# Attention in 64-token chunks with two carried states per tile, and a new order of the work around them

## The chip, the core and the metric

One core of a Trainium2 chip runs the whole program. The metric is the device time of one execution in microseconds (us), lower is better; the median of three runs is given. TensorE does the matrix products, VectorE and ScalarE read their results from the accumulation memory (PSUM, eight banks of 512 fp32 values per partition), GpSimd scatters rows with indirect DMAs, SyncE issues plain DMAs. Every engine runs its own list of instructions in order, and waits on semaphores that the others count up. In the profile TensorE is PE, VectorE DVE, ScalarE ACT, GpSimd POOL.

## The reference

Two residual blocks on X of shape (2, 2048, 256). The first is linear attention with 16 heads of width 16; the second routes each token to 4 of 32 experts, beside a shared expert. The change is in the first block alone:

```python
K = X.reshape(B, L, H, d)          # X here is the layer-normed input, B=2, L=2048, H=16, d=16
Q = rms_norm_multihead((X @ Wq.T).reshape(B, L, H, d), q_norm_w)
V = rms_norm_multihead((X @ Wv.T).reshape(B, L, H, d), v_norm_w)
W = jnp.cumsum(jnp.einsum('blhd,blhe->blhde', K, V), axis=1)    # a running 16x16 state per head
out = jnp.einsum('blhd,blhde->blhe', Q, W).reshape(B, L, D)
x = x + out
```

## The kernel before, in words

The 4096 tokens are 32 tiles of 128. Each engine runs a function `step` once per round; in round i the block `tile_of(k)` works on tile i-k, so a round does one stage of several tiles. The order of the blocks in `step` is the order on that engine, written by hand; nothing reorders it. Channels come in two groups (g) of 128, each of four blocks (j) of 32 channels, which is two heads (r).

For a tile t the stages are, with their lines on TensorE:

- `xn`, the normed tile (ScalarE L517), is transposed (L785), and copied to `xnT` (ScalarE L533). The QV product makes Q and V before their norm, 512 columns in bank `pQV` (L828, two products).
- The norm of Q and V: squares on ScalarE (`sq`, L571), sums per head on VectorE (L1152), logarithm and exponential on ScalarE (L594, L602: a first guess of the root), then three small VectorE operations (L1191, L1202, L1216) give the factors `rr`. VectorE scales Q to `qn` (L1234) and V to `vp` (L1240).
- `qn` is transposed (L817), ScalarE makes from it `qm` (Q masked to one head of each pair, L556) and `qT` (L562).
- The scores, key by query within the tile, are products of 32 rows by 128 columns (L795) into the four banks `pS0` to `pS3`. A causal mask `tri` is applied in three banks by VectorE (L1089), in the fourth by a ScalarE copy (L527) and a GpSimd operation (L482).
- The output of the tile is the product of `qT` with the state carried so far, `w_bd` (L869), plus the masked scores times V (L888), both in bank `pO`. The state sum is added to in bank `pT1` (L877), and VectorE masks it into `w_bd` (L1180) for the next tile.
- ScalarE scales the output to `oT` (L614), TensorE transposes it (L803), VectorE adds it to x (L1113). After that come the second norm and the router of the experts (L774, L838, L846, L858 and many small VectorE operations), and GpSimd scatters each tile's rows four times (L467).

On TensorE the order in a round is: L774, L785, L795 (tile i-2), L803 (tile i-3), L817 (tile i-1), L828 (tile i), router, L869, L877, L888 (tile i-2). On ScalarE `oT` of tile i-3 is the last thing in a round, behind the logarithm and the guess of tile i-1.

Then come the shared expert and 144 blocks of the routed experts, and the sums of their outputs, which the change leaves as they are.

## Time and profile before

| | |
|---|---|
| median of 3 runs | 559.55 us (555.07 to 562.66) |
| the profiled execution: its own time | 559.33 us |
| its span, first to last instruction | 557.4 us |
| PE busy | 527.4 us (95%) |
| DVE / ACT / POOL busy | 382.2 / 376.5 / 331.8 us |
| attention stage | about 10 to 215 us of the span |

The profile is one execution. Times are microseconds from the span's start, unless marked ns. A matrix product of fp32 operands shows as two instructions (x16 for eight products), a transpose as one. "128*32" beside a matrix product is the shape of the part of the array it uses, rows by columns; several such parts can hold products at the same time. Durations of neighbours on an engine may overlap, so what an instruction takes of its engine's time is better read from one start to the next.

### The profile page before, as it was taken

The page shows a single profiled execution, that of the slowest core. Times are in us where ns is not written, and L with a number is a line of the kernel's source. Part 1 is how long each engine was busy: PE and PEld are TensorE (multiplying, and loading weights), DVE is VectorE, ACT ScalarE, POOL GpSimd, SP SyncE. Part 2 cuts the span into 40 slices and gives each one's busy share as a digit, 9 for nine tenths or more (in the row PEclk, how much of TensorE's full clock was granted, in tenths as well). Part 3 has the DMA queues.
Part 4 walks back from the last instruction along what each step waited for, and adds up shares of the span by engine and source line. Part 5 has one row for each costly group of instructions (what it writes and reads, how often), then busy time and mean ns, then how long its engine had stood idle before and what let it go on. Part 6 is the DMA issues. An engine that isn't in the chain of part 4 may idle for free.

```text
span 557.4 us, 18176 instructions
## 1 busy us (share of the span) xinstructions
PE 527.4 (95%) x5177; PEld 383.1 (69%) x5177; DVE 382.2 (69%) x1354; ACT 376.5 (68%) x1258; POOL 331.8 (60%) x367
## 2 busy tenths in 40 slices
PE   6798999999999999699999999999999999997996
PEld 2355666666666665357998988999999995544554
DVE  7698999999999996664444444444444446744786
ACT  2687899988989985402766766777677776653452
POOL 6010377776777777771665555666666564446992
PEclk8999999999999999899999999999999999998999
DMA  8998355556456554954676776766666554428999
GB/s 259 316 292 264 125 217 211 187 215 227 186 198 246 188 192 152 366 194 127 195 219 201 221 225 199 214 193 194 194 193 198 180 187 145 143 79 342 408 409 347
DMA packets 65088, 123.29 MB, mean 221 GB/s; under 512 B 9824, under 2 KB 44000, under 8 KB 64992
## 3 DMA queue, kind: packets, MB, share of 16 engines
q1 hardware_dynamic: 47824, 78.07, 44.1%
q0 software_dynamic: 13056, 39.86, 19.2%
q10 hardware_dynamic: 4112, 4.19, 2.3%
q8 instruction: 45, 0.74, 0.6%
q14 instruction: 51, 0.42, 0.3%
HBM read 58.49 MB, written 63.60 MB: 219 GB/s over the span
## 4 chain that ended last, share of the span: by engine, by line
PE 79%; DMA 5%; DVE 4%; issue 4%; ACT 3%; POOL 2%; SPq 1%; ACTq 1%; DVEq 0%; POOLq 0%
PE pS L967 18%; PE pQV L828 10%; PE pS L985 9%; PE pS L741 8%; PE pS L795 5%; PE pO L888 5%; DMA xg<-xs 3%; PE pO L869 3%; PE pT L946 3%; PE pQV L946 2%; PE pQV L757 2%; PE pO L757 2%; PE pT L774 2%; PE pO L803 2%; PE pT L817 1%
## 5 line engine op out<-in xcount | busy, mean ns | idle before, releaser
L495 POOL DMA_INDIRECT ys<-gsh,dst x144 | 138.1, 959 | 108.3 <-ACT gsh L663 86.6
L467 POOL DMA_INDIRECT xs<-xg,posi x128 | 123.8, 967 | 52.1 <-issue 31.4
L967 PE MATMUL pS<-after_a,x2T_all 128*128 128x128 f32 x1024 | 135.5, 276 | 0.0
L967 PEld LDWEIGHTS pS<-after_a,x2T_all 128*128 128x128 f32 x1024 | 124.5, 192 | 0.0
L1375 DVE TENSOR_TENSOR after_a<-after_a,pS 128x128 f32<-128x128 f32 x144 | 41.5, 288 | 79.9 <-ACT after_a L651 76.1
L1346 DVE COPY x2T_all<-w 128x512 f32 x144 | 63.9, 444 | 32.9 <-issue 32.5
L985 PE MATMUL pS<-w,after_a 128*128 x256 | 76.7, 381 | 0.0
L1089 DVE TENSOR_TENSOR w<-pS,tri 128x512 f32<-128x512 f32 x96 | 65.1, 679 | 1.0 <-PE pS L795 1.0
L828 PE MATMUL pQV<-w 128*128 128x512 f32 x128 | 63.7, 621 | 0.5 <-ACT w L533 0.5
L663 ACT ACTIVATE gsh<-pS,xg 128x256 f32<-128x256 f32 x128 | 60.6, 474 | 0.4 <-issue 0.4
L662 ACT CAST dst<-xg 128x1 int32 x128 | 24.5, 191 | 45.3 <-PE pS L985 43.3
L741 PE MATMUL pS<-x2T_all,ws 128*128 128x512 f32 x104 | 50.6, 636 | 1.3 <-ACT sg L624 0.7
L651 ACT ACTIVATE after_a<-pS 128x128 f32<-128x128 f32 x144 | 40.1, 279 | 16.5 <-PE pS L967 10.7
L482 POOL TENSOR_SCALAR_AFFINE_SELECT w<-w 128x512 f32<-128x512 f32 x32 | 20.6, 643 | 43.3 <-ACT w L527 43.0
L500 POOL TENSOR_TENSOR w<-w 128x512 f32<-128x512 f32 x32 | 40.7, 1272 | 7.7 <-DMA w<-ys 7.4
L985 PEld LDWEIGHTS pS<-w,after_a 128*128 128x128 f32 x256 | 38.9, 192 | 0.4 <-issue 0.4
L556 ACT ACTIVATE w<-pT,mwq 128x128 f32<-128x128 f32 x128 | 36.8, 379 | 1.9 <-PE pT L817 1.7
L741 PEld LDWEIGHTS pS<-x2T_all,ws 128*128 128x128 f32 x104 | 20.9, 207 | 24.6 <-issue 24.3
L795 PE MATMUL pS<-w 32*128 32x256 f32 x512 | 36.7, 401 | 0.0
L828 PEld LDWEIGHTS pQV<-w 128*128 128x128 f32 x128 | 22.2, 194 | 20.2 <-issue 18.2
L888 PE MATMUL pO<-w 128*32 128x128 f32 x1024 | 34.6, 274 | 1.3 <-POOL w L482 0.6
L647 ACT COPY after_a<-pT 128x256 f32<-128x256 f32 x72 | 26.1, 363 | 11.4 <-PE pT L946 11.3
(221 smaller groups left out, 1019.8 us busy)
## 6 DMA issues: line engine op xcount, KB each, us to landing
xg<-xs SPq DMA_DIRECT2D x128, 160.0 KB, 2.8
ys<-gsh SPq DMA_DIRECT2D x32, 512.0 KB
w<-ys SPq DMA_DIRECT2D x32, 512.0 KB, 15.3
w<-in_L_ffn_W ACTq DMA_DIRECT2D x1, 4096.0 KB, 18.6
out<-xall SPq DMA_DIRECT2D x14, 256.0 KB, 7.2
xs<-padrow SPq DMA_DIRECT2D x32, 80.0 KB
xg<-xs SPq DMA_DIRECT2D x32, 80.0 KB, 2.2
ys<-gsh,dst POOLq DMA_INDIRECT x144
```

The source lines that it names most:

```text
L467: pool.indirect_dma_start(out=xs, out_offset=bass.IndirectOffsetOnAxis(ap=posi[:, a.r8, k:k + 1], axis=0), in_=xr[:, a.r8, :], in_offset=N ...
L495: pool.indirect_dma_start(out=ys, out_offset=bass.IndirectOffsetOnAxis(ap=dst[:, j % 8:j % 8 + 1], axis=0), in_=y[:, j % 8, :], in_offset= ...
L663: act.activation(y[:, a.r8, :], pS[2 + a.b][:, 0:D], ACT.Copy, scale=xg[:, a.r8, bass.ds(e[0] + D, 1)]).then_inc(S["y_done"], 1)
L741: last = pe.matmul(h_bank(g, m, n)[:], ws13[:, k, n, m * P:(m + 1) * P], x2T_all[:, k, g * TG:(g + 1) * TG], start=(k == 0), stop=(k == KC ...
L795: last = pe.matmul(pS[j][:, g * 256:(g + 1) * 256], xnT[32 * j:32 * j + 32, a.r3, g, :], qm[32 * j:32 * j + 32, :, g, :], start=(g == 0), ...
L828: last = pe.matmul(pQV[:], xnT[:, a.r3, k, :], wqv[:, k, :], start=(k == 0), stop=(k == KC - 1))
L888: last = pe.matmul(pO[32 * j:32 * j + 32, g * P:(g + 1) * P], vp[:, a.b, 4 * g + j, r:r + 2, :], s_sb[:, j, g, r, :], start=False, stop=(r ...
L967: last = pe.matmul(pS[a.b][:, n * P:(n + 1) * P], w13_staged(a.t)[:, (2 * k + n) * F:(2 * k + n + 1) * F], xgT[:, a.b, k, :], start=(k == ...
L985: last = pe.matmul(pS[2 + a.b][:, 0:D], geT[:, a.b, :], w2_of(e), start=True, stop=True)
L1089: dve.tensor_tensor(s_sb[:, j].rearrange("p g r l -> p (g r) l"), pS[j][:].rearrange("p (n l) -> p n l", l=P), tri[:].unsqueeze(1).to_broa ...
L1346: dve.tensor_copy(w13_staged(j), w13[:, bass.ds(staged_of(j), 1), :, :, :].rearrange("p a k n f -> p (a k n f)")).then_inc(S["w13_staged"], 1)
L1375: dve.tensor_tensor((ge if mixed(a.t) else geT)[:, a.b, :], sge[:, a.b, :], pS[a.b][:, F:2 * F], ALU.mult).then_inc(S["ge_done"], 1)
```

## The change

Each tile of 128 tokens is treated as two chunks (c) of CH = 64 tokens. Scores are made within a chunk only, so they are half as many: products of 32 rows by 64 columns with 128 streamed columns (L805 of the changed kernel), into the first 256 columns of the four banks, now one tensor `pS_all`. The mask is two VectorE operations of two banks each (L1100); the ScalarE copy and the GpSimd mask are gone. The state is carried twice per tile: `carry(b, 0)` for the first chunk and `carry(b, 1)` for the second, each 128 columns (VectorE, L1114), and `add_to_state` adds one chunk (64 rows) to the sum in `pT1`. The product with the carried states and the product of scores and V are of 64 rows by 32 columns with 64 streamed columns (L880, L890). The output goes to the second halves of banks 2 and 3, the transposed `qn` to that of bank 1 (`pQT`), the transposed output to that of bank 0 (`pOT`); the QV product alternates between the banks `pQV` and `pO`, and is issued in two halves with the transposes of `qn` between them. `xn` has four buffers instead of three. On ScalarE `normalise` and `xr` (L552) move forward, and `oT` moves ahead of the logarithm and the guess. On VectorE `v_done` (scaling V) moves from the end of a round into the next.

TensorE, one round before (in it a tile's router columns, L846 to L858):

```order
L774 MATMUL pT<-ident,xg 128x128 x2
L785 MATMUL pT<-ident,w 128x128 x2
L795 MATMUL pS<-w 128x256 x8
L803 MATMUL pO<-ident,w 128x128 x2
L817 MATMUL pT<-ident,w 128x128 x2
L828 MATMUL pQV<-w 128x512 x2
L846 MATMUL pT<-mask,tri 128x64
L847 MATMUL pT<-mcum,ones 128x64
L858 MATMUL pT<-x2T_all,wg 32x128 x4
L869 MATMUL pO<-w,w_bd 32x128 x8
L877 MATMUL pT<-w 32x32 x8
L888 MATMUL pO<-w 32x128 x16
```

and the same round of the changed kernel, which starts behind the state sum of the first chunk (L763, the row that ends it here):

```order
L781 MATMUL pT<-ident,xg 128x128 x2
L793 MATMUL pT<-ident,w 128x128 x2
L805 MATMUL pS<-w 64x128 x16
L814 MATMUL pQV<-w 128x512
L821 MATMUL pS<-ident,w 128x128 x2
L828 MATMUL pQV<-w 128x512
L834 MATMUL pS<-ident,w 128x128 x2
L854 MATMUL pT<-mask,tri 128x64
L855 MATMUL pT<-mcum,ones 128x64
L865 MATMUL pT<-x2T_all,wg 32x128 x4
L763 MATMUL pT<-w 32x32 x8
L880 MATMUL pS<-w,w_bd 32x64 x16
L890 MATMUL pS<-w 32x64 x32
L763 MATMUL pT<-w 32x32 x8
```

The transposes of the output (L834) have moved behind the QV product, the QV product is split, and the state sum of the second chunk stands ahead of the product with the carried states (L880), that of the next tile's first chunk behind the last product (L890).

ScalarE, the part of a round from the squares on, before:

```order
L571 ACTIVATE w<-pQV 128x512
L576 COPY rk<-pT 128x64
L585 COPY after_a<-pT 128x128
L517 ACTIVATE w<-xall,nb,rr 128x256
L594 ACTIVATE lnm<-ss,eps_col 128x34
L602 ACTIVATE guess<-lnm 128x34
L614 ACTIVATE w<-pO,wvc 128x128 x2
L533 COPY w<-pT 128x256
```

and in the changed kernel:

```order
L569 ACTIVATE w<-pQV 128x512
L574 COPY rk<-pT 128x64
L583 COPY after_a<-pT 128x128
L590 ACTIVATE w<-pS,wvc 128x128 x2
L599 ACTIVATE lnm<-ss,eps_col 128x34
L607 ACTIVATE guess<-lnm 128x34
L531 COPY w<-pT 128x256
```

The two operations that make `oT` (L614, now L590) have moved from behind the guess to ahead of the logarithm (L594, now L599).

The core of the diff:

```diff
-        pS = [pb(f"pS{j}") for j in range(4)]
+        pS_all = ctx.enter_context(nc.psum_tensor("pS", [P, 4, 512], F32))
+        pS = [pS_all[:, j, :] for j in range(4)]
+        pQT, pOT = pS_all[:, 1, 256:512], pS_all[:, 0, 256:512]
+        pO_chunks = pS_all[:, 2:4, 256:256 + KC * CH].rearrange("p c (g l) -> p c g l", g=KC)
...
+        def carry(b, c):
+            return w_bd[:, b, c * P:(c + 1) * P].rearrange("p (g j e) -> p g j e", g=KC, j=2)
...
-                if (a := tile_of(2)) is not None:
-                    pool_wait(S["s_copied"], banks_copied(a.t) + 1)
-                    v = s_sb[:, 1].rearrange("p g r l -> p (g r) l")
-                    pool.affine_select(out=v, in_=v, compare_op=ALU.is_ge, fill=0.0, base=0,
-                                       pattern=[[0, 4], [1, P]], channel_multiplier=-1).then_inc(S["masked_pool"], 1)
...
-                if (a := tile_of(3)) is not None:
-                    copy_scores(a, 1)
+                if (a := tile_of(0)) is not None and a.t > 1:
+                    normalise(a.t)
...
+                if (a := tile_of(3)) is not None:
+                    wait(act, S["o_ps"], a.t + 1)
+                    wait(act, S["ot_ps"], a.t)
+                    if a.t == 0:
+                        act.wait_ge(S["wc_in"], 64)
+                    for g in range(KC):
+                        last = act.activation(oT[:, g, :].rearrange("p (c l) -> p c l", c=2), pO_chunks[:, :, g, :], ACT.Copy,
+                                              scale=wvc[:, g:g + 1])
+                    last.then_inc(S["oT_done"], 1)
                 if (a := tile_of(1, LAG)) is not None:
...
+            def add_to_state(a, c):
+                wait(pe, S["v_done"], a.t + 1)
+                wait(pe, S["carried"], states_summed(a.t, c))
+                for g in range(KC):
+                    for j in range(4):
+                        last = pe.matmul(pT1[32 * j:32 * j + 32, g * 2 * d:(g + 1) * 2 * d],
+                                         xn[c * CH:(c + 1) * CH, a.r4, g * P + 32 * j:g * P + 32 * j + 32],
+                                         vp[c * CH:(c + 1) * CH, a.b, 4 * g + j, 0:3:2, :],
+                                         start=(a.t % NTB == 0 and c == 0 and g == 0), stop=True, skip_group_check=True)
+                last.then_inc(S["state_ps"], 1)
...
                     wait(pe, S["qm_done"], a.t + 1)
-                    wait(pe, S["masked"], banks_masked(a.t))
-                    wait(pe, S["s_copied"], banks_copied(a.t))
+                    wait(pe, S["qT_done"], a.t + 1)
+                    wait(pe, S["oT_done"], a.t)
+                    wait(pe, S["x2_done"], a.t - 1)
                     for g in range(KC):
+                        for c in range(2):
+                            for j in range(4):
+                                last = pe.matmul(pS[j][c * CH:(c + 1) * CH, g * P:(g + 1) * P],
+                                                 xnT[32 * j:32 * j + 32, a.r3, g, c * CH:(c + 1) * CH],
+                                                 qm[32 * j:32 * j + 32, :, g, c * CH:(c + 1) * CH],
+                                                 start=(g == 0), stop=True, skip_group_check=True)
+                    last.then_inc(S["scores_ps"], 1)
...
+                if (a := tile_of(0)) is not None:
+                    wait(pe, S["xnT_done"], a.t + 1)
+                    wait(pe, S["qn_done"], a.t - 1)
+                    wait(pe, S["v_done"], a.t - 1)
+                    pe.matmul((pQV, pO)[a.b][:], xnT[:, a.r3, 0, :], wqv[:, 0, :], start=True, stop=False)
...
                         keep_busy(2, 512)
                     wait(pe, S["qn_done"], a.t + 1)
-                    wait(pe, S["x2T_done"], a.t - 3)
-                    wait(pe, S["xnT_done"], a.t + 2, NT)
+                    wait(pe, S["masked"], scores_masked(a.t - 1) + 1)
                     for g in range(KC):
-                        last = pe.transpose(pT0[:, g * P:(g + 1) * P], qn[:, a.b, g * P:(g + 1) * P], ident[:])
+                        last = pe.transpose(pQT[:, g * P:(g + 1) * P], qn[:, a.b, g * P:(g + 1) * P], ident[:])
                     last.then_inc(S["qT_ps"], 1)
...
+                    pe.matmul((pQV, pO)[a.b][:], xnT[:, a.r3, 1, :], wqv[:, 1, :], start=False, stop=True).then_inc(S["qv_ps"], 1)
+                if (a := tile_of(3)) is not None:
+                    wait(pe, S["oT_done"], a.t + 1)
+                    wait(pe, S["masked"], scores_masked(a.t + 1) + 1, scores_masked(NT))
+                    wait(pe, S["x2_done"], a.t)
+                    for g in range(KC):
+                        last = pe.transpose(pOT[:, g * P:(g + 1) * P], oT[:, g, :], ident[:])
...
+                if (a := tile_of(2)) is not None and a.t < NT - 1:
+                    add_to_state(a, 1)
                 if (a := tile_of(2)) is not None:
                     wait(pe, S["qT_done"], a.t + 1)
-                    wait(pe, S["state_done"], a.t)
-                    wait(pe, S["x2_done"], a.t)
+                    wait(pe, S["carried"], states_summed(a.t, 1))
+                    wait(pe, S["masked"], scores_masked(a.t + 1))
                     for g in range(KC):
+                        for turn in range(2):
+                            for j in range(4):
+                                i = j // 2
+                                c = (i + turn) % 2
+                                last = pe.matmul(pO_chunks[32 * j:32 * j + 32, c, g, :], carry(a.b, c)[i * CH:(i + 1) * CH, g, j % 2, :],
+                                                 qT[i * CH:(i + 1) * CH, a.b, g, c * CH:(c + 1) * CH],
+                                                 start=(g == 0), stop=False, skip_group_check=True)
                     last.then_inc(S["o1_ps"], 1)
                 if (a := tile_of(2)) is not None:
-                    wait(pe, S["v_done"], a.t + 1)
-                    wait(pe, S["masked"], banks_masked(a.t + 1))
-                    wait(pe, S["masked_pool"], banks_copied(a.t + 1))
+                    pe.wait_ge(S["o1_ps"], a.t + 1)
                     for g in range(KC):
                         for r in range(2):
+                            for c in range(2):
+                                for j in range(4):
+                                    last = pe.matmul(pO_chunks[32 * j:32 * j + 32, c, g, :],
+                                                     vp[c * CH:(c + 1) * CH, a.b, 4 * g + j, r:r + 2, :],
+                                                     s_sb[c * CH:(c + 1) * CH, j, g, r, :],
+                                                     start=False, stop=(r == 1), skip_group_check=True)
                     last.then_inc(S["o_ps"], 1)
+                if (a := tile_of(1)) is not None:
+                    add_to_state(a, 0)
+                if (a := tile_of(2)) is not None and a.t == NT - 1:
+                    pe.wait_ge(S["carried"], states_summed(NT - 1, 1))
+                    shared_half(1, 1, 0)
...
-            def mask_scores(a, j):
-                wait(dve, S["scores_ps"], 4 * a.t + j + 1)
+            def mask_scores(a, half):
+                banks = slice(2 * half, 2 * half + 2)
+                wait(dve, S["scores_ps"], a.t + 1)
                 wait(dve, S["o_ps"], a.t)
+                dve.tensor_tensor(s_sb[:, banks].rearrange("p j g r l -> p j (g r) l"),
+                                  pS_all[:, banks, 0:4 * CH].rearrange("p j (n l) -> p j n l", l=CH),
+                                  tri[:, 0:CH].unsqueeze(1).unsqueeze(1).to_broadcast([P, 2, 4, CH]), ALU.mult).then_inc(S["masked"], 1)
+
+            def carry_state(t, c):
+                if c == 0:
+                    wait(dve, S["state_ps"], states_summed(t))
+                    wait(dve, S["o1_ps"], t - 1)
+                else:
+                    wait(dve, S["state_ps"], states_summed(t, 1))
+                    wait(dve, S["o1_ps"], t - 1)
+                if c == 0 and t % NTB == 0:
+                    dve.memset(carry(t % 2, 0), 0.0).then_inc(S["carried"], 1)
+                else:
+                    dve.tensor_tensor(carry(t % 2, c),
+                                      pT1[:, 0:KC * 2 * d].rearrange("p (g e) -> p g e", g=KC).unsqueeze(2).to_broadcast([P, KC, 2, 2 * d]),
+                                      head_mask[:, :, 0:CH].rearrange("p g (j e) -> p g j e", j=2), ALU.mult).then_inc(S["carried"], 1)
 
             def step(tile_of):
                 if (a := closing(tile_of(9))) is not None:
...
+                if (a := tile_of(2)) is not None:
+                    wait(dve, S["rms_done"], a.t + 1)
+                    wait(dve, S["o_ps"], a.t - 1)
+                    wait(dve, S["state_ps"], states_summed(a.t - 1))
+                    dve.tensor_tensor(vp[:, a.b, :, 0:3:2, :], (pQV, pO)[a.b][:, D:2 * D].rearrange("p (n r e) -> p n r e", r=2, e=d),
+                                      rr[:, a.b, H:2 * H].rearrange("p (n r) -> p n r", r=2).unsqueeze(3).to_broadcast([P, NP_, 2, d]),
+                                      ALU.mult).then_inc(S["v_done"], 1)
+                if (a := tile_of(3)) is not None:
+                    carry_state(a.t, 1)
+                if (a := tile_of(3)) is not None:
+                    mask_scores(a, 1)
...
+                if (a := tile_of(3)) is not None and a.t < NT - 1:
+                    carry_state(a.t + 1, 0)
```

## Rows read from the trace of the kernel before

**Rows 1.** Windows: length, busy us of PE, PEld, DVE, ACT, POOL, clock, DMA, GB/s

```profile
100.00:120.00 20.00, 19.98 (x326) 13.20 (x314) 19.54 (x91) 18.02 (x63) 14.48 (x16) 1.00 0.55 202
...
220.00:240.00 20.00, 14.76 (x48) 7.02 (x45) 13.76 (x75) 8.44 (x27) 14.95 (x16) 0.83 0.94 334
```

**Rows 2.** Chain of waits, 82.3 to 198.4 us, by line

```profile
by line: PE pQV L828 30.4%; PE pS L795 17.6%; PE pO L888 15.8%; PE pO L869 8.2%; PE pT L774 6.4%; PE pO L803 6.0%; PE pT L817 3.7%; PE pT L785 3.6%; PE pT L858 3.1%; PE pT L877 2.0%; PE pT L846 1.6%; PE pT L838 1.5%; PE pT L847 0.2%; issue 
```

**Rows 3.** Line L785, 80 to 200 us: durations, first and last start

```profile
L785 PE MATMUL pT<-ident,w x40: 272/273/273, 82.3 to 198.4; 128*128 128x128 f32 x40
```

**Rows 4.** Timeline of PE, 133 to 141.4 us: start, us, instruction

```profile
133.05 1.96 PE L828 MATMUL pQV<-w 128*128 128x512 f32 x4
135.01 0.19 PE L846 MATMUL pT<-mask,tri 128*128 128x64 f16 x1
...
135.40 0.62 PE L869 MATMUL pO<-w,w_bd 128*32 128x128 f32 x16
135.84 0.31 PE L877 MATMUL pT<-w 128*32 128x32 f32 x16
135.96 1.06 PE L888 MATMUL pO<-w 128*32 128x128 f32 x32
136.95 0.44 PE L774 MATMUL pT<-ident,xg 128*128 128x128 f32 x2
...
137.54 1.15 PE L795 MATMUL pS<-w 32*128 32x256 f32 x16
138.62 0.43 PE L803 MATMUL pO<-ident,w 128*128 128x128 f32 x2
138.89 0.38 PE L817 MATMUL pT<-ident,w 128*128 128x128 f32 x2
139.22 1.96 PE L828 MATMUL pQV<-w 128*128 128x512 f32 x4
141.02 0.35 PE L838 MATMUL pT<-after_a 128*128 128x64 f32 x2
141.30 0.32 PE L869 MATMUL pO<-w,w_bd 128*32 128x128 f32 x4
```

**Rows 5.** Timeline of ACT, 136.3 to 138.6 us

```profile
136.85 0.31 ACT L594 ACTIVATE lnm<-ss,eps_col 128x34 f32<-128x34 f32 x1
137.19 0.23 ACT L602 ACTIVATE guess<-lnm 128x34 f32<-128x34 f32 x1
137.33 0.61 ACT L614 ACTIVATE w<-pO,wvc 128x128 f32<-128x128 f32 x2
137.83 0.37 ACT L533 COPY w<-pT 128x256 f32<-128x256 f32 x1
```

**Rows 6.** Timeline of DVE, 137.3 to 145.5 us

```profile
137.46 0.20 DVE L1191 SCALAR_TENSOR_TENSOR newt<-ss,guess 128x34 f32<-128x34 f32 x1
...
138.35 0.40 DVE L1234 TENSOR_TENSOR w<-pQV,rr 128x256 f32<-128x256 f32 x1
...
139.17 0.68 DVE L1089 TENSOR_TENSOR w<-pS,tri 128x512 f32<-128x512 f32 x1
139.77 0.41 DVE L1113 TENSOR_TENSOR xall<-xall,pO 128x256 f32<-128x256 f32 x1
...
143.58 0.20 DVE L1191 SCALAR_TENSOR_TENSOR newt<-ss,guess 128x34 f32<-128x34 f32 x1 [0.16 <-ACT guess L602]
...
144.38 0.42 DVE L1234 TENSOR_TENSOR w<-pQV,rr 128x256 f32<-128x256 f32 x1
```

**Rows 7.** Groups of DVE by line and shape, 80 to 200 us: busy us, mean ns

```profile
L1089 DVE TENSOR_TENSOR w<-pS,tri 128x512 f32<-128x512 f32 x58 | 39.4, 679 | 0.0
...
L1240 DVE TENSOR_TENSOR w<-pQV,rr 128x256 f32<-128x256 f32 x20 | 8.3, 415 | 0.0
L1180 DVE TENSOR_TENSOR w_bd<-pT,head_mask 128x256 f32<-128x256 f32 x19 | 7.7, 404 | 0.0
...
L1161 DVE TENSOR_TENSOR vm<-mask,rk 128x64 f32<-128x64 f16 x10 | 2.2, 216 | 0.0
```

More of the change, by code:

```diff
@@ L65, in build @@
     HB = P // 2
+    CH = P // 2
     NM = E // 2
@@ L522, in _ @@
                 act.copy(wqv[:, k, :], (pT0, pT1)[k][:]).then_inc(S["wt_done"], 1)
-            def copy_scores(a, j):
-                wait(act, S["scores_ps"], 4 * a.t + j + 1)
-                wait(act, S["o_ps"], a.t)
-                act.copy(s_sb[:, j].rearrange("p g r l -> p (g r l)"), pS[j][:]).then_inc(S["s_copied"], 1)
             def step(tile_of):
@@ L561, in step @@
                     wait(act, S["o1_ps"], a.t - 1)
[L562 to L567 removed]
+                    act.copy(qT[:, a.b], pQT.rearrange("p (g m) -> p g m", g=KC)).then_inc(S["qT_done"], 1)
                 if (a := tile_of(1)) is not None:
@@ L607, in step @@
                                    accum_out=se[:, a.pb, 0:1]).then_inc(S["exp_done"], 1)
-                if (a := tile_of(3)) is not None:
-                    wait(act, S["o_ps"], a.t + 1)
-                    wait(act, S["ot_ps"], a.t)
-                    if a.t == 0:
-                        act.wait_ge(S["wc_in"], 64)
-                    for g in range(KC):
-                        last = act.activation(oT[:, g, :], pO[:, g * P:(g + 1) * P], ACT.Copy, scale=wvc[:, g:g + 1])
-                    last.then_inc(S["oT_done"], 1)
             pipelined(NT, 8, step)
@@ L871, in step @@
-                    last.then_inc(S["o1_ps"], 1)
-                if (a := tile_of(2)) is not None and a.t < NT - 1:
-                    wait(pe, S["v_done"], a.t + 1)
-                    wait(pe, S["state_done"], a.t)
-                    for g in range(KC):
-                        for j in range(4):
-                            last = pe.matmul(pT1[32 * j:32 * j + 32, g * 2 * d:(g + 1) * 2 * d],
-                                             xn[:, a.r3, g * P + 32 * j:g * P + 32 * j + 32], vp[:, a.b, 4 * g + j, 0:3:2, :],
-                                             start=(a.t % NTB == 0 and g == 0), stop=True, skip_group_check=True)
-                    last.then_inc(S["state_ps"], 1)
+                        for turn in range(2):
[5 more added lines that the diff above has]
+                                                 start=(g == 0), stop=False, skip_group_check=True)
@@ L881, in step @@
+                    last.then_inc(S["o1_ps"], 1)
                 if (a := tile_of(2)) is not None:
-                    wait(pe, S["v_done"], a.t + 1)
-                    wait(pe, S["masked"], banks_masked(a.t + 1))
-                    wait(pe, S["masked_pool"], banks_copied(a.t + 1))
+                    pe.wait_ge(S["o1_ps"], a.t + 1)
                     for g in range(KC):
                         for r in range(2):
-                            for j in range(4):
-                                last = pe.matmul(pO[32 * j:32 * j + 32, g * P:(g + 1) * P],
-                                                 vp[:, a.b, 4 * g + j, r:r + 2, :], s_sb[:, j, g, r, :],
-                                                 start=False, stop=(r == 1), skip_group_check=True)
@@ L1135, in step @@
                     stats1(n.t)
+                if (a := tile_of(4)) is not None:
+                    wait(dve, S["ot_ps"], a.t + 1)
+                    dve.tensor_tensor(xall[:, a.t, :], xall[:, a.t, :], pOT, ALU.add).then_inc(S["x2_done"], 1)
+                if (a := tile_of(4)) is not None:
+                    wait(dve, S["x2_done"], a.t + 1)
+                    dve.bn_stats(st2[:], xall[:, a.t, :]).then_inc(S["stats2"], 1)
+                if (a := tile_of(4)) is not None:
+                    wait(dve, S["stats2"], a.t + 1)
+                    dve.bn_aggr(mv2[:, a.t % 8, :], st2[:]).then_inc(S["mean2"], 1)
                 if (a := closing(tile_of(8))) is not None:
```

141 lines of the change are left out of this document (43 added, 98 removed).

## The prediction

> **What bounds the kernel now.** I read the windows first. In the attention stage PE, DVE and ACT are busy for 19.98, 19.54 and 18.02 of 20 us, POOL for 14.48, at a granted clock of 1.00 [rows 1]: two full engines, so busy time alone doesn't name the bound. The chain of waits from 82 to 198 us runs on PE alone [rows 2]. PE's transposes of `xn` give the pace: 20 rounds begin between 82.3 and 198.3 us, 6.10 us each [rows 3]. Then the timelines, for what stands between the engines. The normed Q ends on DVE at 138.35 + 0.40 = 138.75 [rows 6], and its transposes start at 138.89 [rows 4]: 0.14 us later, and nothing keeps PE but this. The next round's logarithm needs the QV product that follows. So the loop QV product, squares, norm, `qn`, transposes, QV product is as tight as the two engines, and all three sit near 6.10 us.
>
> The profiled execution took 559.33 us, 0.2 below the median of 559.55; the sum is made against 559.33. The attention stage is 32 rounds and a few to fill and drain, of which I count 28 as steady. What a measurement can tell from no change is about 2%, or 11.2 us: 0.4 us a round.
>
> **The change part by part.**
>
> *Less work on DVE.* Two mask operations replace three. One takes 679 ns [rows 7] and holds DVE for 0.60 from its start to the next one's (139.17 to 139.77) [rows 6]; the new ones also write 512 elements per partition, so I price them alike: -0.60. One state operation of 256 elements (404 ns) becomes two of 128; between the 216 ns of 64 elements and 404 [rows 7] I take 280 each, less the 0.08 by which neighbours overlap (139.17 + 0.68 against 139.77): +0.08. The residual add, its statistics, their mean and the variance now follow one another directly, each needing the one ahead. Dependent neighbours don't overlap: on ACT the guess starts 0.03 after the logarithm ends (136.85 + 0.31, 137.19) [rows 5]. I put 0.12 on each of the three: +0.36. DVE's sum is 6.10 - 0.60 + 0.08 + 0.36 = 5.94; without the last term, 5.58.
>
> *Less work on ACT and POOL.* A copy of 512 columns and a POOL mask go. Neither is where the chain runs, and I count nothing; four scatters a round stay.
>
> *PE.* Scores stream half as much, and so does the product with V, if its parts run side by side. 32 instructions of L888 take 0.99 to the next line's start (135.96 to 136.95), 16 of L869 take 0.44 (135.40 to 135.84) [rows 4]; so 0.88 of the 0.99 is streaming and 0.11 the change of the array's shape. New L890 has twice the instructions with half the columns. With eight parts at once (two by rows, four by columns) it streams in 0.44, with four in 0.88. The rows show four parts by columns (L888) and four by rows (L795), never both. I take eight, since L795 and L888 each reach four. L880 stays at 0.44, because each column group serves one row half only. A second state sum is one more L877: 0.12 (135.84 to 135.96).
>
> The Trainium skill, "TensorE: Matmul & The Clock Gate", Part 3 (Packing small matmuls), says that row and column parts compose, with 10.6 times the speed for 16; by that, eight run at once. No run here shows it yet.
>
> L890 now waits for L880's own result, which nothing on PE did before. A result lands 0.18 after its streaming (L869's 0.62 against 0.44), and a wait takes 0.14 to release PE (above): +0.32, with nothing between. PE's sum is 6.10 - 0.44 - 0.44 + 0.12 + 0.32 + 0.05 = 5.71. The 0.05 is one more change of shape in every other round.
>
> *The waits that are new, which decide.* The transposes of `qn` write into bank 1, where scores lie, and wait for the first mask (`masked`), which DVE does behind `qn`. And ACT now makes `oT` ahead of the logarithm: behind the waiting `oT` stand logarithm and guess, for which DVE waits. This closes a loop that takes one round:
>
> - first mask 0.68 [rows 6], release of PE 0.14: 0.82
> - transposes of `qn`, and of `oT`: a pair takes 0.27 (138.62 to 138.89) behind a change of shape, 0.22 without (2 x 0.11): 0.50
> - second half of the QV product: half of 1.80 (139.22 to 141.02): 0.90
> - router: 0.28 in one round (141.02 to 141.30), 0.39 (135.01 to 135.40) in the other, whose QV product also takes 0.16 more (1.96 from 133.05): mean 0.42, and 0.05 for the shape: 0.47
> - state sum 0.12, L880 0.44, its own wait 0.32
> - L890 0.44, its last result 0.18: 0.62
> - ACT: release 0.04, `oT` 0.50 (137.33 to 137.83), logarithm to guess 0.34 (136.85 to 137.19), guess to L1191 0.27 (137.19 to 137.46) [rows 5, 6]: 1.15
> - DVE from L1191 to L1234: 0.89 and 0.80 in two rounds: 0.85
> - from L1234 to the mask: 0.82 (138.35 to 139.17) less the scaling of V that left this place (415 ns less 0.08), and a little less every other round: 0.45
>
> Sum: 0.82 + 0.50 + 0.90 + 0.47 + 0.12 + 0.44 + 0.32 + 0.62 + 1.15 + 0.85 + 0.45 = 6.64 us. It is longer than either engine's sum, so it sets the pace: DVE then waits for the guess some 0.7 us a round, ACT for the last product. 6.64 - 6.10 = 0.54, times 28 is 15.1: **574.5 us**. Each term is from a row, but no row shows this loop. With releases and tails a quarter shorter it would be 6.4 (568), with a little disorder 6.8 (579).
>
> Splitting the QV product hides its first half behind the masks; without it the loop would be 0.9 longer. That is counted, and is why I don't put the kernel further out. The start-up loses two tiny constants, under 1 us. In the end of the stage the shared expert's products fill PE as before.
>
> **The rivals.**
>
> *Eight parts don't run at once.* Row parts of the same column group share the way out. Then L890 is 0.88: 7.08 a round, 0.98 x 28 = 27: 587. For it: no row has both kinds. Against: each kind alone runs at four. 14%.
>
> *Small instructions keep the large ones' pace.* L888 starts one per 0.99/32, or some 28 ns with the shape taken off. If 64-column instructions kept that, L890 would take 1.76, L880 0.88: 8.4 a round, and some 624 us. Against it stands L877: 16 starts in 0.12 us, 8 ns each. 1%. The same page of the Trainium skill ("Back-to-back issue gap" and the section on 56 ns) says that starts are never nearer than 25 ns; the trace disagrees for parts side by side, with 8.
>
> *The loop is not the bound, the engines' sums are.* This is the other side. Decisive is when ACT reaches `oT`: if PE is early enough that `o_ps` is up when ACT gets there, logarithm and guess aren't held. That needs the loop under 5.94, 0.7 less than my sum. ACT has shed 0.6 of work, and half of PE's terms are inferred. Then DVE's 5.94 sets the pace: -0.16 x 28 = -5: 554.5, no change that can be told. 20%. If the dependent neighbours cost nothing, 5.58: -0.52 x 28 = -15: 544.5. Full engines like DVE at 98% make that thinkable, since every cut of busy time there shows. 13%.
>
> *The clock falls.* With PE idle near 1 us a round its busy share is some 85%. At 220 to 240 us, where PE was busy for 14.76 of 20 us with idle stretches, the granted clock averaged 0.83 [rows 1]. If half the stage dropped so, PE's streaming of some 3 us a round would cost 20%: +8 over my sum, 583. 4%.
>
> **How the numbers follow.** My loop has 48%, with 566 to 580 as its own range; 8 of the 48 lie under 570.7. Slower by over 2%: 40 + 14 + 1 + 4 = 59, faster 13, within 2% 20 + 8 = 28. The range goes from 549 to 590: it leaves out the 13 at 544 and a few at the upper end.
>
> **What would show it.** Right: ACT idle ahead of L590 for `o_ps`, DVE idle ahead of L1217 for the guess, both over 0.4 us a round; L793 starting 6.5 to 6.8 us apart; about 0.3 between the last start of L880 and the first of L890; L890 in 0.45 to 0.55; DVE busy under 18.5 of 20 us. Wrong: DVE busy for over 19 of 20 us and no wait of ACT at L590, at under 6 us a round; or L890 in 0.88, with the same loop.

## The result

The changed kernel takes 635.22 us in the median of 4 runs (632.81 to 638.15), the kernel before 560.7 beside it: a ratio of 1.135, with a 95% interval from 1.125 to 1.145. The forecast was 574.5, with a range of 549 to 590. The sign was right, and the size was wrong by a factor of five: 75 us in place of 15.

The page of the changed kernel. First busy time and instructions, then two of the lines by slices, the queue that brings instructions, and the chain of waits by engine:

```profile
PE 550.0 (87%) x7737; PEld 392.1 (62%) x7737; DVE 379.5 (60%) x1356; ACT 361.1 (57%) x1226; POOL 311.1 (49%) x335
...
PE   6767887888787877768799999999999999998896
...
q8 instruction: 66, 1.08, 0.7%
...
PE 72%; issue 10%; DVE 5%; DMA 4%; SPq 4%; ACT 4%; POOL 0%; DVEq 0%; ACTq 0%; POOLq 0%
```

Nearly all the time lies in the attention stage: its last product with V starts at 286.6 us, where it started at 215.3, which is 71 of the 74 us. The windows there, with the columns of [rows 1]:

```profile
100.00:120.00 20.00, 17.19 (x391) 10.06 (x391) 14.18 (x65) 11.85 (x41) 8.40 (x9) 0.83 0.40 147
140.00:160.00 20.00, 16.53 (x460) 10.04 (x448) 16.41 (x75) 14.32 (x53) 10.26 (x11) 1.00 0.40 147
160.00:180.00 20.00, 15.21 (x501) 9.97 (x499) 14.59 (x64) 12.26 (x45) 7.74 (x9) 1.00 0.49 182
```

Where [rows 1] had PE and DVE full, no engine is full now, at full clock too, and the clock falls in between. The same stretch of the chain by line as in [rows 2], 82.3 to 198.4 us:

```profile
by line: issue 18.0%; PE pS L890 11.8%; PE pS L805 7.9%; PE pO L814 7.9%; PE pS L880 6.1%; PE pQV L828 5.8%; PE pS L821 4.8%; PE pO L828 4.6%; PE pQV L814 4.2%; PE pT L763 4.0%; DVE w L1100 3.5%; PE pT L781 2.9%; PE pS L834 2.5%; PE pT L865
```

"issue", time in which PE waits for nothing that the profile shows, has become the largest item. What PE waited for from 60 to 290 us (total us, times, longest; the five largest of ten lines):

```profile
PE pS L890 <- issue: 10.2, 7, 2.4
PE pS L805 <- issue: 9.2, 9, 2.4
PE pT L763 <- issue: 7.2, 4, 2.4
PE pS L821 <- DVE w L1100: 7.0, 11, 1.6
PE pS L890 <- PE pS L880: 2.3, 8, 0.4
```

Only the last two lines are waits that the prediction had named. The others are one kind of event, here in PE's timeline (start us, us, instruction, idle before it):

```profile
161.46 0.86 PE L890 MATMUL pS<-w 64*32 64x64 f32 x64
162.12 0.33 PE L763 MATMUL pT<-w 64*32 64x32 f32 x16
162.51 0.41 PE L781 MATMUL pT<-ident,xg 128*128 128x128 f32 x2
162.76 0.38 PE L793 MATMUL pT<-ident,w 128*128 128x128 f32 x2
163.23 0.46 PE L805 MATMUL pS<-w 32*64 32x128 f32 x11
166.01 0.66 PE L805 MATMUL pS<-w 32*64 32x128 f32 x21 [2.33 <-issue]
```

PE stops inside the scores, after 11 of 32 matmuls that all have the same inputs ready, and goes on 2.33 us later. The program has no wait between these matmuls. In the window from 163 to 167 us the list of queues has one packet of the instruction queue (packets, MB, share), 16 KB, and it starts at 163.68 by the records:

```profile
q8 instruction: 1, 0.02, 1.5%
```

This suggests that PE ran out of instructions; e6 and the count below bear it out. The stage has 46 such transfers (20 to 300 us), the kernel before 26 (20 to 231 us).

### The profile page after: what moved, and what is told of

It is laid out like the page before. It is cut to its first block, busy times and chain, and to the rows that moved or that the text cites. A ratio compares the mean times of both kernels' runs of the same rounds, so it can differ in the third digit from the quotient of the medians.

```text
span 631.1 us, 23229 instructions
## 1 busy us (share of the span) xinstructions
PE 550.0 (87%) x7737; PEld 392.1 (62%) x7737; DVE 379.5 (60%) x1356; ACT 361.1 (57%) x1226; POOL 311.1 (49%) x335
## 4 chain that ended last, share of the span: by engine, by line
PE 72%; issue 10%; DVE 5%; DMA 4%; SPq 4%; ACT 4%; POOL 0%; DVEq 0%; ACTq 0%; POOLq 0%
PE pS L975 17%; PE pS L993 8%; PE pS L738 7%; PE pS L890 5%; PE pS L805 3%; PE pS L880 3%; PE pO L814 3%; PE pQV L828 2%; PE pQV L814 2%; PE pT L954 2%; PE pO L828 2%; PE pQV L954 2%; PE pQV L754 2%; PE pT L763 2%; PE pS L821 2%
## 5 line engine op out<-in xcount | busy, mean ns | idle before, releaser
L498 POOL DMA_INDIRECT ys<-gsh,dst x144 | 138.6, 962 | 105.3 <-ACT gsh L660 83.4
L559 ACT ACTIVATE w<-pS,mwq 128x128 f32<-128x128 f32 x128 | 36.5, 368 | 32.8 <-PE pS L821 32.1
L1100 DVE TENSOR_TENSOR w<-pS,tri 128x512 f32<-128x512 f32 x64 | 43.6, 682 | 16.8 <-PE pS L805 16.5
L590 ACT ACTIVATE w<-pS,wvc 128x128 f32<-128x128 f32 x64 | 20.0, 364 | 52.8 <-PE pS L890 48.7
L890 PE MATMUL pS<-w 64*32 64x64 f32 x2048 | 31.8, 227 | 14.5 <-issue 10.2
L805 PE MATMUL pS<-w 32*64 32x128 f32 x1024 | 29.2, 320 | 16.8 <-issue 13.9
L890 PEld LDWEIGHTS pS<-w 64*32 64x32 f32 x2048 | 24.5, 107 | 21.6 <-issue 11.6
L805 PEld LDWEIGHTS pS<-w 32*64 32x64 f32 x1024 | 19.0, 152 | 25.0 <-issue 25.0
L644 ACT COPY after_a<-pT 128x256 f32<-128x256 f32 x72 | 26.2, 363 | 11.6 <-PE pT L954 11.6
```

The lines of the kernel that those rows point to most:

```text
L498: pool.indirect_dma_start(out=ys, out_offset=bass.IndirectOffsetOnAxis(ap=dst[:, j % 8:j % 8 + 1], axis=0), in_=y[:, j % 8, :], in_offset= ...
L805: last = pe.matmul(pS[j][c * CH:(c + 1) * CH, g * P:(g + 1) * P], xnT[32 * j:32 * j + 32, a.r3, g, c * CH:(c + 1) * CH], qm[32 * j:32 * j ...
L890: last = pe.matmul(pO_chunks[32 * j:32 * j + 32, c, g, :], vp[c * CH:(c + 1) * CH, a.b, 4 * g + j, r:r + 2, :], s_sb[c * CH:(c + 1) * CH, ...
L1100: dve.tensor_tensor(s_sb[:, banks].rearrange("p j g r l -> p j (g r) l"), pS_all[:, banks, 0:4 * CH].rearrange("p j (n l) -> p j n l", l=C ...
```

## The experiments

Two sets of numbers must be kept apart. In some sessions, on the same chip too, the kernel before took 700 to 710 us and not 560. It has no profile there, but those of other kernels in such sessions (c3, e10) show engines idle at places where they aren't otherwise: in e10, the kernel nearest to it, ScalarE waits for 36 us from 60 to 260 us, in 11 stops of up to 4.5 us, put down to "remote". Why stays open. A kernel is compared only with kernels of its own kind of session: at 560 are c1, c2, e5, e6, e14 and e15; at 700 to 710 are e1 to e4, e7 to e10, c3 and e11 to e13, told by their ratio to the kernel before.

**Controls.** c1 is the kernel before, c2 and c3 the changed kernel, all unchanged.

> The kernel before, unchanged, for a profile of it on the chip on which the next kernels run. The runs e1 to e4 stood beside a kernel before of 710 us instead of 560, so their chip or its state is another one. A: here either about 560 as at first, or about 710 with PE standing still at places where it did not at first; the trace will show which.

> The changed kernel, unchanged, beside e5 and e6 on one chip. Ratio to the kernel before 1.12 to 1.15, as measured first, if the chip is as at first; if before is at 710 again, then 790 to 810.

> The changed kernel, unchanged, as the control of this group. 635 to 638 if the kernel before shows 560; if it shows 709 as beside e1 to e4 and e7 to e10, then the ratio is open, and e3 and e9 (1.117, 1.119 of before) and e4 (1.099) are read against it.

c1: 560.8 us. c2: 636.7, ratio 1.140 (1.133 to 1.146). c3: 785.9, ratio 1.122 (1.116 to 1.128) at 699.8 for the kernel before. In c2 PE again starts 11 matmuls of the same scores (at 164.24), stands idle for 2.60 us and starts the other 21 at 167.30: the place belongs to the program.

**e6: the old kernel with the new number of instructions.** The decisive run. The excerpts of code here and below are shortened.

```
 # scores, carried product, state sum and product with V: each call
 # in two calls of half the columns, e.g. the product with V
-for j in range(4):
-    matmul(pO[32*j:32*j+32, g*P:(g+1)*P], vp[...], s_sb[:, j, g, r, :])
+for c in range(2):
+    for j in range(4):
+        matmul(pO[32*j:32*j+32, g*P+c*HB : g*P+(c+1)*HB], vp[...], s_sb[:, j, g, r, c*HB:(c+1)*HB])
```

> The kernel before, its order, waits, banks and results kept, with each matmul of the scores, the carried product, the state sum and the product with V cut in two by columns: 40 calls more per tile, as many as the change adds, for the same columns streamed. A (PE stands still for its own instructions): transfers of instructions in the stage from 26 to about 46, stretches of 1 to 2.3 us in which PE waits for nothing shown, 580 to 605. B (the loop of the new order is what costs): no loop is new here, so 560 to 565. D (each small matmul costs more than its columns): L888's and L795's passes themselves grow, 0.99 to 1.3 or more, with no long standing still; 575 to 590.

> The kernel of e2 once more (the kernel before with the scores, the carried product, the state sum and the product with V cut in two by columns: as many PE instructions as in the changed kernel, no other change). Against c1 on the same chip. A: 20 to 45 us more, in stretches in which PE waits for nothing shown beside transfers of instructions. B: no difference. D (each small matmul dearer): 15 to 30 us more, in the passes of L796 and L893 themselves.

e6: 631.0 us, ratio 1.127 (1.124 to 1.130). That is 70 us more with no new wait, no new loop and the same columns: nearly the whole loss of the change (c2: 76). The mechanism is A; the amount is above A's range. B, the loop as the cause of the loss, is out. PE's waits from 20 to 270 us:

```profile
PE pO L893 <- issue: 25.2, 11, 4.7
PE pS L796 <- issue: 15.2, 8, 2.7
```

In c1 (20 to 205 us) PE's issue idle time is 2.1 us in 2 stops. A part is D: the state sum, 0.12 us to the next line in c1, takes 0.33 to 0.50, 0.42 in the mean, and the product with V 1.03 in undisturbed rounds, for 0.99. Such rounds take 6.4 us instead of 6.1. e2, the same kernel at 710, has the ratio 1.068 (1.061 to 1.075): in that kind of session the split alone explains a little over half of the changed kernel's 1.122, and what the rest is was not found.

**e5: the changed kernel with few instructions.** The carried product in 64x64 pieces, and work left out as the expectation says.

```
-for j in range(4):            # carried product: 16 calls a tile
-    i = j // 2
-    matmul(pO_chunks[32*j:32*j+32, c, g, :], carry(..)[i*CH:(i+1)*CH, g, j % 2, :], qT[...])
+for i in range(2):            # 8 calls
+    matmul(pO_chunks[i*CH:(i+1)*CH, c, g, :], carry(..)[i*CH:(i+1)*CH, g, :, :], qT[...])
-for r in range(2):            # product with V
+for r in range(1):
-for g in range(KC): for j in range(4):              # state sum, c == 1
+for g in range(KC if c == 0 else 1): for j in range(4 if c == 0 else 1):
```

> The changed kernel with fewer instructions on PE: the product with the carried state as 8 matmuls of 64x64 in place of 16 of 64x32 (the same values), and, left out of the computation, the r = 1 half of the product with V and all but one matmul of the second half's state sum. That is 31 matmul calls less per tile, 124 of PE's some 370 instructions; every wait and all the work of the other engines stay. A (PE stands still for its own instructions: the profile has 46 transfers of 16,384 bytes of instructions in the attention stage of the changed kernel, against 26, and some 41 us of idle PE beside them): about 31 transfers, the standing still gone but for 5 to 10 us, the half-clock stretches mostly gone with it, loop shorter by 0.5 us a round: 635 - 35 - 8 - 14 = about 578. B (the loop alone is longer than forecast): only the shorter passes count, V 0.33 and the rest 0.15 us a round: -14, about 621. C (the clock alone): between, about 605.

> The kernel of e1 once more (8 calls of 64x64 for the carried product; the r = 1 half of the product with V and all but one matmul of the second half's state sum left out; 124 PE instructions less of some 370 a round). Against c2 on the same chip. A (standing still for instructions): 50 to 60 us less than c2. B (the loop alone): 14 us less. C (clock alone): 30 less.

e5: 581.1 us, ratio 1.040 (1.036 to 1.043), 55.5 us under c2. A had 50 to 60, B 14. 28 transfers in the stage. Its waits from 20 to 222 us:

```profile
PE pS L821 <- DVE w L1100: 13.9, 28, 0.7
PE pT L763 <- DVE w_bd L1114: 2.9, 13, 0.4
PE pS L890 <- issue: 1.7, 1, 1.7
```

With the instructions in time, the wait for the first mask comes forward in 28 rounds. That wait closes the predicted loop, at 6.5 us a round. e1 has the ratio 1.066, where c3 has 1.122.

**e14: 16 of the 40 calls.** Only the product with V is cut, as in e6.

> The kernel before with only the product with V cut in two by columns: 16 calls (64 PE instructions) more per tile, 40% of what e6 added for 70 us. If each additional instruction costs the same: +28, about 588. If it costs only where 256 instructions run in less time than a transfer needs (2.3 to 2.6 us): the densest passage (carried product, state sum, product with V, transposes, scores) then holds 32 + 32 + 128 + 16 + 32 = 240 instructions in some 3.4 us, just about enough time: +5 to +15, 565 to 575.

> The kernel of e13 once more (the kernel before with only the product with V cut in two by columns; 64 PE instructions more per tile). With the kernel before at 560: 588 if each additional instruction costs the same as in e6, 565 to 575 if the cost has a threshold. With the kernel before at 700: as e13, 726.

e14: 578.2 us, ratio 1.035 (1.030 to 1.040): 19 above the 559.0 beside it, between the two forecasts. 12.6 us of issue idle time (31 transfers), and 1.14 instead of 0.99 for the pass of V, 0.15 x 31 = 5. Many rounds keep 6.1. The cost isn't the same for each instruction; but neither does it begin where 256 instructions run in 2.3 to 2.6 us, as the lower forecast had it, since no block of 256 ran in under 3.9 us here (how blocks are counted stands further down). e13 has 1.038.

**e15: the loop opened.** e5 with ScalarE's `oT` behind the guess (e4 does this to the changed kernel).

```
 act: ... lgT copy
-     oT activations (wait o_ps)
      logarithm, nmx, guess
+     oT activations (wait o_ps)
      exp
```

> The kernel of e5 (the r = 1 half of the product with V and all but one matmul of the second half's state sum left out, few instruction stalls, rounds of 6.5 us in the steady part) with ScalarE's oT moved behind the guess. This is the loop of the prediction by itself. If that loop sets the 6.5 (first mask, transposes, QV half, products, oT, logarithm, guess, norm, mask): the round falls to 6.1 to 6.25, 581 to 568-573, and the wait of DVE for the guess goes. If something else sets it: 579 to 583.

> The kernel of e8 once more: that of e5 (581 us with the kernel before at 560; r = 1 half of the product with V and all but one matmul of the second half's state sum left out) with ScalarE's oT behind the guess. If the prediction's loop sets the 6.5 us of a round there: 6.1 to 6.25, 568 to 573. If not: 579 to 583.

> The kernel of e8 and e11 once more (few instructions, oT behind the guess; the r = 1 half of the product with V and all but one matmul of the second half's state sum left out). With the kernel before at 560: 568 to 573 if the prediction's loop sets the 6.5 us a round of e5 (581), 579 to 583 if not. With it at 700: as e8 and e11, no difference from e1.

e15: 588.7 us, ratio 1.053 (1.049 to 1.058), where e5 has 1.040 (1.036 to 1.043): slower by 1.4%, against both forecasts. The waits from 100 to 200 us of the profiled executions (580.5 and 583.5 us) suggest why. First e5, then e15:

```profile
ACT w L590 <- PE pS L890: 10.4, 15, 0.8
DVE newt L1217 <- ACT guess L607: 4.2, 14, 0.5
PE pS L821 <- DVE w L1100: 7.4, 15, 0.7
```

```profile
ACT lnm L590 <- DVE ss L1187: 16.6, 15, 1.2
PE pS L805 <- ACT w L605: 12.1, 15, 1.0
DVE newt L1217 <- ACT guess L598: 3.5, 15, 0.3
```

In e15 the logarithm no longer waits for the product with V. It now waits for the sums of squares, and PE's scores wait for `oT`, whose source lies in the banks that they write. The named loop was closed in e5 (all three waits there in every round or nearly), but a second one, `oT` to scores, was right behind. That this second loop sets e15's time is read from the waits; no run opened it. e8 (1.076) and e11 (1.081) were no faster than e1 (1.066) either.

> The changed kernel with ScalarE's oT moved from ahead of the logarithm to right behind the guess: the loop that the prediction named is opened there (logarithm and guess no longer wait for the product with V). B (loop alone sets the pace, at 8.2 us a round): the loop loses oT 0.50, the release and what was waited for at L590, 0.4 us a round or more: 615 to 624. A (standing still for instructions on top of a loop of about 6.5): the gain is 0.2 to 0.3 us a round where nothing is awaited: 626 to 633, with as many transfers and as much standing still as before.

e4: ratio 1.099 (1.091 to 1.106), where c3 has 1.122 on another chip. By that the same move gains some 2% in the complete changed kernel there; e12 below has the move too and shows no gain, so it isn't settled. It was not run in a session at 560.

**e3, e9, e12: mending the changed kernel.** e3 and e9 move one matmul call; e12 adds e5's 64x64 pieces and e4's move, with nothing left out.

```
 qT transposes
-QV product, second half
 oT transposes, router, state sum, carried product
+QV product, second half
 wait o1_ps; product with V
```

> The changed kernel with the second half of the QV product moved from behind the transposes of qn to between the carried product and the product with V, where PE now waits for its own result (0.29 to 0.40 us a round). Same work, same number of instructions. A: the dense passage of small matmuls is cut by 0.9 us of long ones, in which instructions can arrive: the own wait is hidden (-0.32 x 28 = -9) and part of the standing still: 610 to 618. B (loop alone): -9, about 626. If the squares now come too late for the logarithm: +0.3 us a round, 640 or more.

> The kernel of e3 once more, on a chip as at first: the changed kernel with the second half of the QV product between the carried product and the product with V, in the middle of the dense passage of small matmuls. Against 636.7 for the changed kernel. A: own wait hidden (-0.3 a round) and 0.9 us more time for the next transfer in the dense passage: 605 to 620. Loop alone: 626 to 628. If the squares come too late: 640 or more.

> The changed kernel, complete, with three edits at once: the carried product as 8 calls of 64x64 (32 PE instructions less per tile), the second half of the QV product between the carried product and the product with V, and oT behind the guess. A (instructions late in the dense passage): 42 transfers in the stage instead of 46, own wait hidden, the standing still cut by a third: 600 to 612. Loop alone: 637 - 0.5 x 28 = 623. If neither matters: 635.

e3 1.117 (1.110 to 1.125), e9 1.119 (1.111 to 1.127), e12 1.131 (1.124 to 1.137), against 1.122 for c3. None gains anything that can be told. All ran at 700 to 710 only, where PE in c3 has a wait of another kind (60 to 300 us), so how they would do at 560 stays open:

```profile
PE pS L890 <- remote: 46.4, 7, 7.0
```

**e7: instructions without matmuls.**

```
+for _ in range(4): pe.wait_ge(w_in, 32)     # already satisfied
 last = pe.matmul(...)                        # the 40 calls of e6's four groups
```

> The kernel before with four waits that are already satisfied ahead of each matmul call of the scores, the carried product, the state sum and the product with V: 160 instructions more per tile on PE, as many and at the same places as in e2/e6 (560 to 631 us), but no matmul more. A (PE's instructions don't arrive in time, whatever they are): transfers of instructions in the stage from 26 to about 46, standing still of 1 to 3 us beside them, 600 to 640. D (small matmuls are what costs): 560 to 565. If satisfied waits cost time of their own, the undisturbed rounds grow above 6.1 us, and that is to be taken off.

e7: ratio 1.217 (1.208 to 1.226), and inconclusive on its question. Two waits became one instruction, so 80 were added to a tile and not 160, and each cost PE time itself: the product with V took 3.99 us with 32 of them, 0.99 without, 94 ns each. What it does show: transfers came some 12 us apart, and no two matmuls of the stage started more than 0.9 us apart. At that pace instructions are never late, in that kind of session too.

**e10: the kernel before, with fewer instructions.**

```
-for j in range(4): matmul(pO[32*j:32*j+32, ...], w_bd[:, a.b, at:at+32], qT[...])   # 128x32
+matmul(pO[:, ...], w_bd[:, a.b, g*P:(g+1)*P], qT[...])                              # 128x128
```

> The other direction, on the kernel before: its product with the carried state as 2 matmul calls of 128x128 in place of 8 of 128x32 (the state is stored block-diagonal, zeros included, so the values are the same). 24 PE instructions less per tile, of some 270. L869's pass falls from 0.44 to 0.22 to 0.30 us, since a call of this form (the transposes) takes 0.11 to 0.14. If PE's sum counts in the kernel before: -0.15 x 32 = -5, about 555. If the loop through the normed Q is as tight by itself: the pass lies in it too (state sum, product with V, transposes and QV product are all on PE), so the same; if DVE and ACT bind: 560.

e10: ratio 1.0005 (0.997 to 1.004). No gain, and no version here beats the kernel before. L867's pass took 0.54 to 0.64 us, mostly 0.59 or 0.64, where 0.22 to 0.30 was expected and the eight calls take 0.44 [rows 4]: here one 128x128 call is dearer than four of 128x32 side by side.

## Why the prediction was wrong

**The step that failed** is the one on PE: "New L890 has twice the instructions with half the columns", and with eight parts at once "it streams in 0.44". It priced instructions by the columns that they stream. The change adds 40 calls to a tile, 160 instructions on PE (each call is two weight loads and two matmuls in the records), and their supply was not in the sum. Neither did the rivals have it; *small instructions keep the large ones' pace* came out near the time (624) by a mechanism that did not occur, since L890's 64 starts take 0.66 to 0.71 us in undisturbed rounds and not 1.76.

**How the supply works here.** I counted PE's instructions in the trace from the first that it holds: weight loads, matmuls and the waits between them, in order of their starts. In c2 and e6, 34 pauses of over 1.1 us (1.3 in c2) between two matmul starts have a transfer ahead of them. Ahead of every one of the 34, the number of instructions started is a multiple of 256 plus 193, to the instruction, whatever line that is. The two pauses of c1 stand there too, and the six of e14. A transfer of 16 KB is a block of 256 instructions, and this is the border of the blocks; why it lies at 193 in this count is not shown. From the first border after 20 us to the end of the stage each block has exactly one transfer in it. After a pause PE goes on 2.2 to 3.3 us after that transfer began. So while PE runs one block the next is on its way, and if it isn't there at the border, all of PE stops.

Two times decide, then: how fast PE runs through a block, and how late in it the next one's transfer begins. The changed kernel's dense passage (state sum 32, carried product 64, product with V 128, state sum 32, transposes 8, scores 64) is 328 instructions and runs in 3.25 us, from the first to the last of these lines. That is 256 in 2.5 us, no more than a transfer takes to become usable:

```profile
193.64 0.32 PE L763 MATMUL pT<-w 64*32 64x32 f32 x15
...
194.49 0.86 PE L890 MATMUL pS<-w 64*32 64x64 f32 x64
...
196.26 0.70 PE L805 MATMUL pS<-w 32*64 32x128 f32 x32
196.89 1.12 PE L814 MATMUL pO<-w 128*128 128x512 f32 x2
```

The same passage before has 32 + 32 + 64 + 8 + 32 = 168 from 135.40 to 138.62 [rows 4], 256 in 4.9; a whole block took 6.2 us or more there, and PE paused twice in the stage (c1).

But a transfer doesn't begin with its block. In c1, e6, c2 and e14 it began 0.1 to 8.2 us after the block's first instruction. So 17 of the 34 pauses end blocks that ran for 3.4 to 7.0 us, and the six of e14 end blocks of 5.2 to 5.7 us, where the transfer had begun after 4.2 to 4.9. What sets that start, no run here shows; it is what keeps the cost from following from the number of instructions alone.

The Trainium skill, "Advanced Engine Details and Errata", section "ISA Cache", says that a cache line is 16 KB, which is 256 instructions, and that there are only two of them (beside 32 KB in all, or 128 KB on TensorE). The trace agrees with the line of 256; how many lines there are no run here shows. I had not drawn on it.

**The account.** For each kernel of the 560 sessions, over its stage:

| | c1 before | e14 | e5 | e6 | c2 changed |
|---|---|---|---|---|---|
| calls more per tile | 0 | 16 | 9 | 40 | 40 |
| transfers | 24 | 31 | 28 | 42 | 42 |
| PE idle for issue, us | 2.1 | 12.6 | 2.8 | 41.2 | 35.9 |
| at half clock, us | 0 | 3.4 | 10.2 | 39.1 | 47.9 |
| mean round, us | 6.12 | 6.68 | 6.68 | 8.23 | 8.36 |
| time, us | 560.8 | 578.2 | 581.1 | 631.0 | 636.7 |

For e6: 39 us of pauses, at most 39/2 = 20 from the half clock (1.2 GHz in place of 2.4), and 0.30 x 31 = 9 for the dearer state sum. That makes at most 68 of the 70. For c2: 34 of pauses, at most 24 from the half clock, and the rest of the 76, 18 or more, is the loop and what the engines lose while they find step again. The half clock is an upper bound, since PE was idle in part of that time. Each of c2's nine stretches at half clock begins between 1.2 us before and 2.0 us after the end of a pause of 1.6 us or more, but the clock alone was never separated from the pauses.

**What held, and what was short.** The named loop is there, but it was priced at 6.64 us and is longer. It was summed from the first mask and the transposes of `qn` (L821) to those of the next round. In nine rounds of the changed kernel (four in the first profile, five in c2; the first round apart) that hold neither a pause of over 0.3 us at a border nor half clock, it took 6.7 to 7.2 us, 7.0 in the mean. Here it took 158.76 - 151.74 = 7.02:

```profile
151.74 0.41 PE L821 MATMUL pS<-ident,w 128*128 128x128 f32 x2
...
153.49 0.62 PE L880 MATMUL pS<-w,w_bd 64*32 64x64 f32 x30
154.29 0.91 PE L890 MATMUL pS<-w 64*32 64x64 f32 x64 [0.18 <-PE pS L880]
...
158.76 0.41 PE L821 MATMUL pS<-ident,w 128*128 128x128 f32 x2 [0.36 <-DVE w L1100]
```

```profile
155.57 0.62 ACT L590 ACTIVATE w<-pS,wvc 128x128 f32<-128x128 f32 x2 [1.38 <-PE pS L890]
```

```profile
156.70 0.20 DVE L1217 SCALAR_TENSOR_TENSOR newt<-ss,guess 128x34 f32<-128x34 f32 x1 [1.04 <-ACT guess L607]
```

The mis-sized term is the product with V and its way to `oT`: from L890's first start to L590's, 1.28 us here (154.29 to 155.57) and 0.89 in most rounds, where 0.44 + 0.18 + 0.04 = 0.66 was said. The terms behind it on ACT (1.13 for 1.11), on DVE (1.24 for 1.30) and the mask with its release (0.82) fit.

Of the signs: ACT idle ahead of L590 and DVE ahead of L1217 by over 0.4 us: right. About 0.3 between the last start of L880 and the first of L890: right, 0.29 in most rounds. L890 in 0.45 to 0.55: wrong, 0.66 to 0.71, so 64 starts of 11 ns instead of 7; eight parts do run side by side (one after the other in fours would be 0.88), but not free. DVE under 18.5 of 20 us: right, 14.2 to 16.4, though the pauses have a share in it. L793 6.5 to 6.8 apart: no; the mean is over 8. *The clock falls* was right as an event and mostly wrong in its cause: in c2 it is pauses of some 2 us. Idle time of a loop can do it too: e15 has no such pause at a border, and still 11.6 us at half clock.

What the loop is worth can be read from e5, which has few pauses: 6.5 against 6.12 in 28 rounds is 11 us, with a product with V that is 0.3 shorter. With 7.0 us, as in the nine rounds, it would be (7.0 - 6.12) x 28 = 25, an estimate, where the forecast had 15. That alone would have given some 584, still inside the range: what took the time out of it is the supply of instructions. The loop isn't one that can be opened at one place (e15). And since e6 has no such loop and loses 70 all the same, loop and pauses don't simply add.

## What to carry to other kernels

Count the instructions of each engine beside its columns: halving the columns of a matmul to save streaming doubles what has to be fetched. Where 256 instructions run before the next block's transfer has begun and landed (here it became usable 2.2 to 3.3 us after its start, and the start itself came up to some microseconds into the block), PE stands still and can then pay again in clock. In the kernel before, with 6.2 us or more to a block, that happened twice in a stage; in e14, with 3.9 or more, six times; in e6, with blocks down to 1.8, 18 times. A cut in two that changes nothing else (e6) prices this before the real change is written. When a pause stands in the middle of a group of equal instructions, look at the instruction queue, not at the semaphores, and count whether the pauses lie a multiple of 256 instructions apart.

## What was not expected of the hardware

- A transfer of instructions is 16 KB, occupies its queue for 0.9 to 2.0 us, and PE goes on 2.2 us after its start at the earliest (c2, e6).
- All 34 long pauses of c2 and e6, in two different programs, stand at the same place of a block of 256 instructions, to the instruction.
- The transfer of the next block begins anywhere from 0.1 to 8.2 us into the running one (c1, e6, c2, e14); why is open.
- Matmuls of parts of 64 rows by 32 columns, 64 columns streamed, in eight places of the array start 11 ns apart (0.71 us for L890's 64). Those of parts of 128 rows by 32 columns start 13 ns apart with 16 columns streamed (e6's state sum, 0.42 us for 32), and 8 ns apart with 32 streamed (c1, 0.12 us for 16).
- Two satisfied waits in one instruction cost PE 94 ns (e7: 3.99 - 0.99 us for 32 of them).
- The kernel before took 560 us in one session and 710 in another on the same chip. The changed kernel has 66 transfers of instructions in both kinds of session (c2, c3). Not explained.
